# One semaphore for both producers of a scattered pair, and the other gathers held back behind the second expert's two tiles

## The chip, the cores and the metric

The kernel runs on one core of a Trainium2 chip. The metric is device time in microseconds for one execution; lower is better. Before the change, three runs took 111.3, 111.6 and 111.39 us, a median of 111.39.

## The reference, cut to what matters

Two layers, all in float32, with B = 4 sequences of S = 256 tokens and width H = 256.

```python
x = x + xattn(layernorm(x), ctx, Wq, bq, Wk, bk)    # attention among the 256 context rows mixes the columns of x
x = x + ffn(layernorm(x), gate_weight, wi, wo)

# ffn: T = 1024 tokens, E = 8 experts, capacity C = 160 rows for each
logits = tokens @ gate_weight.T
probs = softmax(logits)
mask = one_hot(argmax(logits), E)
ranks = cumsum(mask, axis=0) - 1                # place of a token in its expert's queue
mask = mask * (ranks < C)                       # tokens beyond the capacity are dropped
hmid = gelu(dispatch @ wi)                      # (8, 160, 256) x (8, 256, 1024)
eout = hmid @ wo                                # (8, 160, 1024) x (8, 1024, 256)
out = sum over experts of weight * eout         # each token gets its own row back
```

## The kernel before, in words

The program is written out by hand: each engine has its own list of instructions, and semaphores join them. Tokens are handled in 8 tiles of 128 rows, two tiles (a pair b, tiles 2b and 2b+1) for each sequence.

**Front part.** Attention and the first residual give `rows[:, n, 0:256]`, the new x of tile n. Beside it in `rows` stand four more columns: mean, reciprocal standard deviation, token index and softmax sum. For each pair VectorE ranks the tokens (`ranks`, `place`, L556 to L566) and writes `slot`, the place of each token's row in a table `slots_dram` in HBM of 8 x 160 rows of 1040 bytes. ScalarE's `expz(b)` (L394 to L399) writes the softmax sum. POOL makes the reciprocal standard deviation in `second_rstd(b)` (L300 to L304) and writes the rows of tile n to their slots with an indirect DMA, `scatter(n)` (L306 to L316). POOL's order is written out in L318 to L340: second_rstd(0), shifted_input(7), scatter(0), second_rstd(1), scatter(1), second_rstd(2), scatter(2), scatter(3), second_rstd(3), scatter(4) to scatter(7). The table is first filled with a constant row (L226, semaphore `filled`). Before the first scatter of a pair POOL waits for the slots (`slot_done`) and for the softmax sums (`zs_done`); scatter(0) waits for `filled` too. All eight scatters add to `scattered`.

**Expert 0** does not need the table: TensorE gathers its tokens by one-hot matrix products (`disp`), and the expert's first product starts from there.

**The other experts** read the table. SP waits for `scattered` (L232) and issues, one after the other and without a further wait: got_one (ranks 0 to 127 of expert 1, 130 KB), got_zero (expert 0, needed only for its output), got_main (experts 2 to 7, 780 KB in one DMA, 128 runs of 6240 bytes), rest_here[1] (ranks 128 to 159 of experts 4 to 7), the four stores of x to the output (`x1_out`), two more pieces of ranks 128 to 159 for the outputs (`last_slots`), and the weights of experts 3 to 7 (L233 to L242). ScalarE issues rest_here[0] (ranks 128 to 159 of experts 0 to 3) itself, in its own order: ahead of the third gelu of expert 0, so after the second (L443 to L449). The weights of experts 0 to 2 were loaded in the front part.

**Order on VectorE and TensorE.** `load_tile(i)` (L692 to L706) takes input tile i from the gathered rows and normalises it into `stok`; TensorE turns it with two transposes, `dT(i)` (L918 to L926, the matmuls of L778), and `load_tileT(i)` copies it to `dispT`. Input tile 0 is expert 1's (waits for got_one), tile 1 is rest_here[0]'s, tiles 2 and 3 are experts 2 and 3 (wait for got_main), tile 4 is rest_here[1]'s. `mm1(e)` is the first product of expert e: 16 block products, each of which the profile shows as two matmuls, in three groups of 12, 12 and 8 matmuls (L928 to L944). `mm2(e)` is the second product (L952 to L962). The transposes are placed inside: dT(0) and dT(1) ahead of the last quarter of mm2(0), dT(2) between the second and the third group of mm1(1), dT(3) ahead of mm1(2). The order is (L985 to L998):

```python
            mm1(0)
            mm2(0, next(outs), then=INS_AT[0])
            mm1(1, then=INS_AT[1])
            for s in range(2, E + 1):
                for i in INS_AT[s]:
                    dT(i)
                if s < E:
                    mm1(s)
                mm2(s - 1, next(outs))
```

`out_tile(n)` (L720 to L740) scales and adds the output of an expert's tile, and POOL scatters it to the output rows (L342 to L348); the first of these waits until all of `x1_out` has landed.

Of the kernel before, what the change touches and what calls it, by code (L numbers as in the profile page):

```python
# [5 lines left out]
ALU = mybir.AluOpType  # L6
ACT = mybir.ActivationFunctionType
AX = mybir.AxisListType
# [5 lines left out]
B = 4  # L14
# [15 lines left out]
MEAN, RSTD, INDEX, WEIGHT = H, H + 1, H + 2, H + 3  # L30
# [17 lines left out]
def xattn_moe(nc, x_in_v, xT_v, ctxT_v, small_v, wi_v, wo_v, out):  # L48
# [5 lines left out]
    with ExitStack() as stack:  # L54
        def sb(name, shape, dt=F32):
            return stack.enter_context(nc.sbuf_tensor(name, shape, dt))

        def sem(name):
            return stack.enter_context(nc.semaphore(name))
# [12 lines left out]
        def part(at, size, pattern, **sizes):  # L72
# [16 lines left out]
        rows = sb("rows", [P, NT, ROW])  # L89
# [30 lines left out]
        ranked = sb("ranked", [P, B, 2, E])  # L120
        slot = sb("slot", [P, NT], I32)
# [34 lines left out]
        fill_done, filled = sem("fill_done"), sem("filled")  # L156
# [8 lines left out]
        scaled_done, logits_done, lmax_done = sem("scaled_done"), sem("logits_done"), sem("lmax_done")  # L165
        below_done, val_done, vmax_done, mask_done = (sem("below_done"), sem("val_done"), sem("vmax_done"),
                                                      sem("mask_done"))
        rk_done, rank_read, slot_f_done, slot_done = (sem("rk_done"), sem("rank_read"), sem("slot_f_done"),
                                                      sem("slot_done"))
        bn2_done, st2_done, veps2_done = sem("bn2_done"), sem("st2_done"), sem("veps2_done")  # L170
        rstd2_done, zs_done, share_done = sem("rstd2_done"), sem("zs_done"), sem("share_done")
        warm_done = sem("warm_done")
        index_done, end_done = sem("index_done"), sem("end_done")
        tok_done, onehot_done = sem("tok_done"), sem("onehot_done")
# [2 lines left out]
        got_zero, got_one, got_main = sem("got_zero"), sem("got_one"), sem("got_main")  # L177
        got_rem = [sem(f"got_rem{r}") for r in range(STACKS)]
        rest_here = [sem(f"rest_here{r}") for r in range(STACKS)]
# [15 lines left out]
        @block.sync  # L195
        def _(sp):
            def context(i):
                a, z = CHUNKS[i]
                sp.dma_start(ctxT[:, a:z, :], ctxT_v[a:z].rearrange("b c s -> c b s")).then_inc(ctx_here[i], 16)  # L199

            def inputs(i):
                sp.dma_start(x_sb[:, 4 * i:4 * i + 4, :], x_in_v[i]).then_inc(x_here[i], 16)  # L202

            def turned_inputs(i):
                sp.dma_start(xT[:, 2 * i:2 * i + 2, :, :], xT_v[i]).then_inc(xT_here[i], 16)

            def weights(e):
                sp.dma_start(wi_sb[:, e, :, :], wi_v[e]).then_inc(wi_here[e], 16)
                sp.dma_start(wo_sb[:, e, :, :], wo_v[e]).then_inc(wo_here[e], 16)

            def last_slots(r):
                first = r * PER_STACK
                sp.dma_start(got[:, E + r, :],
                             by_rank[P:CAP, first:first + PER_STACK, :].rearrange("q j w -> j q w")
                             ).then_inc(got_rem[r], 16)

            context(0)
            context(1)
            inputs(0)
            context(2)  # L220
            turned_inputs(0)
            inputs(1)
            turned_inputs(1)

            sp.wait_ge(fill_done, 2)
            sp.dma_start(slots_dram.rearrange("(n p) r -> p n r", p=P),  # L226
                         fill[:, None, :].to_broadcast([P, E * CAP // P, ROW])).then_inc(filled, 16)
            weights(0)
            weights(1)
            weights(2)  # L230

            sp.wait_ge(scattered, 16 * NT)  # L232
            sp.dma_start(got[:, 1, :], by_rank[0:P, 1, :]).then_inc(got_one, 16)  # L233
            sp.dma_start(got[:, 0, :], by_rank[0:P, 0, :]).then_inc(got_zero, 16)
            sp.dma_start(got[:, 2:E, :], by_rank[0:P, 2:E, :]).then_inc(got_main, 16)
            sp.dma_start(rest[:, 1, :], by_rank[P:CAP, PER_STACK:E, :]).then_inc(rest_here[1], 16)
            for b in range(B):
                sp.dma_start(out_v[b], rows[:, 2 * b:2 * b + 2, 0:H]).then_inc(x1_out, 16)
            last_slots(0)
            last_slots(1)  # L240
            for e in range(3, E):
                weights(e)  # L242

        @block.gpsimd
        def _(pool):
# [53 lines left out]

            def second_rstd(b):  # L300
                pool.wait_ge(veps2_done, b + 1)
                pair = slice(2 * b, 2 * b + 2)
                nc.gpsimd.tensor_tensor(rows[:, pair, RSTD], rows[:, pair, RSTD], minus_half[:, 0:2],
                                        ALU.pow).then_inc(rstd2_done, 1)  # L304

            def scatter(n):  # L306
                if n == 0:
                    pool.wait_ge(slot_done, 1)
                    pool.wait_ge(zs_done, 2)
                    pool.wait_ge(filled, 16)  # L310
                elif n % 2 == 0:
                    pool.wait_ge(zs_done, n + 2)
                    pool.wait_ge(slot_done, n // 2 + 1)
                nc.gpsimd.indirect_dma_start(  # L314
                    slots_dram, bass.IndirectOffsetOnAxis(ap=slot[:, n:n + 1], axis=0), rows[:, n, :], None,
                    bounds_check=last_slot, oob_is_err=False).then_inc(scattered, 16)  # L316
# [9 lines left out]
            shifted_input(5)  # L326
            shifted_input(6)
            second_rstd(0)
            shifted_input(7)
            scatter(0)  # L330
            second_rstd(1)
            scatter(1)
            second_rstd(2)
            scatter(2)
            scatter(3)
            second_rstd(3)
# [23 lines left out]
        def _(act):  # L360
# [33 lines left out]
            def expz(b):  # L394
                act.wait_ge(below_done, b + 1)
                act.wait_ge(rstd2_done, b + 1)
                for n in range(2 * b, 2 * b + 2):
                    nc.scalar.activation(ez[:, n, :], below[:, b, n % 2, :], ACT.Exp, scale=rows[:, n, RSTD:RSTD + 1],  # L398
                                         accum_out=rows[:, n, WEIGHT:WEIGHT + 1]).then_inc(zs_done, 1)  # L399

            def token(n):

# [17 lines left out]
            exp(3)  # L420
            at(2)
            expz(0)
            token(0)
            at(3)
            expz(1)
            token(1)
            token(2)
            token(3)
            expz(2)
            token(4)  # L430
            token(5)
# [20 lines left out]
        def _(dve):  # L452
# [8 lines left out]
            def pair_of(b):  # L461
                return slice(2 * b, 2 * b + 2)
# [99 lines left out]
            def place(b):  # L562

                dve.wait_ge(rank_read, b + 1)
                nc.vector.tensor_reduce(slot_f[:, pair_of(b)], ranked[:, b, :, :], AX.X, ALU.max).then_inc(slot_f_done, 1)
                nc.vector.tensor_reduce(slot[:, pair_of(b)], ranked[:, b, :, :], AX.X, ALU.max).then_inc(slot_done, 1)  # L566

            def pick(n):

# [66 lines left out]
            ranks(0)  # L636
            summed(1)
            place(0)
            largest(1)
            x1(3)  # L640
# [18 lines left out]
            pick(0)  # L659
            pick(1)  # L660
            place(1)
            value(2)
            pick(2)
# [14 lines left out]
            ranks(2)  # L678
            first(3)
            place(2)  # L680
            chosen(3)
            pick(4)
# [347 lines left out]
```

## Time and profile before

| | |
|---|---|
| median of three runs | 111.39 us (111.3 to 111.6) |
| the profiled execution | 112.25 us |
| its span, first to last instruction | 110.5 us |
| TensorE matmuls busy | 102.0 us, 92% of the span |
| VectorE, ScalarE, POOL busy | 34.6, 31.5, 31.1 us |
| mean DMA rate over the span | 233 GB/s |

The profile shows one execution by the hardware profiler. PE is TensorE, PEld its weight loads, DVE VectorE, ACT ScalarE, POOL GpSimd, SP the engine that issues most DMAs. An engine name with q (SPq, ACTq, POOLq) is that engine's sequencer: the time of a DMA issue there is the issue alone, and not the transfer. L233 is line 233 of the kernel. Times are from the first instruction on.

### The profile page before, as it was taken

What the parts mean: (1) busy time and instruction counts of PE and PEld (TensorE: products, weight loads), DVE (VectorE), ACT (ScalarE), POOL (GpSimd) and SP (SyncE); (2) the same over time, 40 slices, a digit from 0 to 9 for tenths busy, and PEclk for the clock granted to TensorE, in tenths of its full rate; (3) what the DMA queues carried; (4) which work ended last, traced back from release to release, by engine and by line L of the source; (5) the groups of instructions that cost most, each with busy time, mean ns of one, the idle gap of its engine ahead of it and who ended that gap; (6) DMA issues with size and microseconds to landing.
All of it is one profiled execution on the core that took longest, in us unless ns stands there. A gap on an engine that the chain in (4) does not pass through costs nothing.

```text
span 110.5 us, 1990 instructions
## 1 busy us (share of the span) xinstructions
PE 102.0 (92%) x758; PEld 89.8 (81%) x758; DVE 34.6 (31%) x151; ACT 31.5 (29%) x81; POOL 31.1 (28%) x55
## 2 busy tenths in 40 slices
PE   5988999999799999999999999999999999999900
PEld 5565888678689989999999998669999999888800
DVE  0019899999930041800420400220020010012110
ACT  3247675367534302332031041002303204100000
POOL 5501388586775000030210210303002011031540
PEclk9999999999999999999999999999999999999995
DMA  2799999999973499999999999950001001001100
GB/s 76 225 336 371 352 296 421 427 415 414 423 278 120 122 279 371 304 309 411 428 424 415 427 421 424 427 190 16 0 0 41 6 0 47 0 0 46 56 3 3
DMA packets 7986, 25.77 MB, mean 233 GB/s; under 512 B 928, under 2 KB 4773, under 8 KB 5928
## 3 DMA queue, kind: packets, MB, share of 16 engines
q1 hardware_dynamic: 6664, 23.24, 56.3%
q0 software_dynamic: 880, 2.12, 5.2%
q10 hardware_dynamic: 432, 0.27, 0.9%
q8 instruction: 6, 0.10, 0.4%
q14 instruction: 4, 0.03, 0.1%
HBM read 21.14 MB, written 4.76 MB: 234 GB/s over the span
## 4 chain that ended last, share of the span: by engine, by line
PE 78%; DMA 6%; DVE 4%; ACT 4%; issue 3%; SPq 1%; POOL 1%; ACTq 0%; DVEq 0%
PE ps L781 71%; DMA shared<-in_ctxT 6%; PE ps L871 3%; ACT shared L406 2%; PE ps L778 2%; PE ps L824 1%; ACT ez L398 1%; DVE rows L516 1%; POOL out L353 1%; SPq L199 1%; DVE nmax L493 1%; ACT attended L366 0%; DVE stats L580 0%; SPq L202 0%; DVE y_end L757 0%
## 5 line engine op out<-in xcount | busy, mean ns | idle before, releaser
L781 PE MATMUL ps<-wo_sb,shared 128*32 128x128 f32 (+2 forms) x320 | 36.6, 337 | 0.0
L781 PE MATMUL ps<-shared,wi_sb 128*128 128x160 f32 x256 | 36.3, 299 | 0.3 <-issue 0.3
L781 PEld LDWEIGHTS ps<-shared,wi_sb 128*128 128x128 f32 x256 | 35.1, 190 | 0.6 <-issue 0.4
L781 PEld LDWEIGHTS ps<-wo_sb,shared 128*32 128x32 f32 (+1 forms) x320 | 29.4, 142 | 5.1 <-issue 1.0
L448 ACT ACTIVATE shared<-ps 128x480 f32<-128x480 f32 (+1 forms) x24 | 12.6, 526 | 48.2 <-PE ps L781 48.2
L346 POOL DMA_INDIRECT out<-y,got x9 | 8.7, 971 | 59.3 <-DVE y L739 44.1
L739 DVE SCALAR_TENSOR_TENSOR y<-ps,share,got 128x256 f32<-128x256 f32 x9 | 4.4, 484 | 48.1 <-PE ps L781 24.7
L314 POOL DMA_INDIRECT slots_dram<-rows,slot x8 | 8.2, 1028 | 4.0 <-issue 1.4
L781 PE MATMUL ps<-attended,shared 128*128 128x272 f32 x32 | 8.4, 402 | 0.2 <-ACT attended L366 0.2
L781 PEld LDWEIGHTS ps<-attended,shared 128*128 128x128 f32 x32 | 5.7, 189 | 1.4 <-ACT attended L366 0.3
L871 PE MATMUL ps<-shared 128*128 128x160 f32 x32 | 5.3, 309 | 0.6 <-ACT shared L406 0.6
L781 PE MATMUL ps<-shared,small 128*128 128x256 f32 (+1 forms) x12 | 5.1, 542 | 0.8 <-DMA shared<-in_ctxT 0.7
L705 DVE TENSOR_SCALAR stok<-got 128x256 f32<-128x256 f32 x7 | 2.7, 415 | 9.0 <-DMA got<-slots_dram 9.0
L871 PEld LDWEIGHTS ps<-shared 128*128 128x128 f32 x32 | 4.6, 190 | 1.0 <-ACT shared L406 0.8
L472 DVE BATCH_NORM_STATS2 stats<-shared 128x6 f32<-128x256 f32 x8 | 3.0, 414 | 6.9 <-DMA shared<-in_x 6.9
L781 PEld LDWEIGHTS ps<-shared,small 128*128 128x128 f32 x12 | 2.4, 230 | 2.8 <-DMA shared<-in_ctxT 1.4
L824 PEld LDWEIGHTS ps<-turner,shared 128*128 128x128 f32 x32 | 4.2, 190 | 0.3
L824 PE MATMUL ps<-turner,shared 128*128 128x136 f32 x32 | 4.4, 279 | 0.0
L384 ACT ACTIVATE shared<-ps,nmax 128x256 f32<-128x256 f32 x8 | 3.7, 469 | 2.0 <-DVE nmax L493 2.0
L297 POOL TENSOR_SCALAR shared<-shared,shift 128x256 f32<-128x256 f32 x8 | 4.0, 508 | 0.4 <-DVE shift L488 0.4
L781 PE MATMUL ps<-shared 128*128 128x256 f32 x16 | 4.0, 384 | 0.0
L366 ACT ACTIVATE attended<-ps 128x264 f32<-128x264 f32 x8 | 3.0, 390 | 3.6 <-PE ps L824 3.5
(82 smaller groups left out, 77.4 us busy)
## 6 DMA issues: line engine op xcount, KB each, us to landing
wi_sb<-in_wi SPq DMA_DIRECT2D x8, 1024.0 KB, 16.6
wo_sb<-in_wo SPq DMA_DIRECT2D x8, 1024.0 KB, 16.7
slots_dram<-fill SPq DMA_DIRECT2D x1, 1300.0 KB, 13.1
shared<-in_x SPq DMA_DIRECT2D x2, 512.0 KB, 7.4
shared<-in_xT SPq DMA_DIRECT2D x2, 512.0 KB, 8.2
out<-rows SPq DMA_DIRECT2D x4, 256.0 KB, 5.4
got<-slots_dram SPq DMA_DIRECT2D x1, 780.0 KB, 6.6
got<-slots_dram SPq DMA_DIRECT2D x4, 130.0 KB, 2.4
```

The costliest lines, as they stand in the source:

```text
L297: nc.gpsimd.tensor_scalar(x_sb[:, n, :], x_sb[:, n, :], 1.0, shift1[:, n:n + 1], ALU.mult, ALU.add).then_inc(xs_done, 1)
L314: nc.gpsimd.indirect_dma_start(slots_dram, bass.IndirectOffsetOnAxis(ap=slot[:, n:n + 1], axis=0), rows[:, n, :], None, bounds_check=last_ ...
L346: nc.gpsimd.indirect_dma_start(out_rows, bass.IndirectOffsetOnAxis(ap=got[:, t, INDEX:INDEX + 1].bitcast(I32), axis=0), y[:, n % 2, :], No ...
L366: return nc.scalar.activation(dst, src, ACT.Copy)
L384: nc.scalar.activation(att[:, b, m, :], p_en[b][:, m * S:(m + 1) * S], ACT.Exp, bias=nmax[:, n:n + 1], accum_out=esum[:, n:n + 1]).then_in ...
L448: nc.scalar.activation(gelu[:, e % RING, a:z, :], p_h[j][:, 0:(z - a) * CAP], ACT.Gelu).then_inc(gelu_done, 1)
L472: nc.vector.bn_stats(stats[:, 0, n, :], x_sb[:, n, :]).then_inc(bn1_done, 1)
L705: nc.vector.tensor_scalar(stok[:, i % 2, :], row[:, 0:H], row[:, MEAN:MEAN + 1], row[:, RSTD:RSTD + 1], ALU.subtract, ALU.mult).then_inc(s ...
L739: nc.vector.scalar_tensor_tensor(y[:, n % 2, :], p_o[n % 2][:, 0:H], share[:, t:t + 1], got[:, t, 0:H], ALU.mult, ALU.add).then_inc(y_done, 1)
L781: return nc.tensor.matmul(dst, lhsT, rhs, start=(k == 0), stop=last)
L824: last = nc.tensor.matmul(p_at[c][:, E + m * P:E + m * P + HALF], att[:, b, m, c * P:(c + 1) * P], turner[:, b % 2, m * HALF:(m + 1) * HAL ...
L871: last = nc.tensor.matmul(p_disp[c], tok[:, n, c * P:(c + 1) * P], onehot[:, n, :], start=(n == 0), stop=(n == NT - 1))
```

## The change

Three edits. The semaphores `zs_done` and `slot_done` are replaced by one for each pair, `row_ready[b]`, to which ScalarE adds twice and VectorE once, and the scatter of an even tile waits for 3 of it. The wait for `filled` moves from scatter(0) to second_rstd(0). On SP, two waits are put in behind the issue of got_one: one for got_one itself and one for rest_here[0]; got_zero, got_main and everything behind them are issued after that.

```diff
--- before.py
+++ after.py
@@ -165,10 +165,10 @@
         scaled_done, logits_done, lmax_done = sem("scaled_done"), sem("logits_done"), sem("lmax_done")
         below_done, val_done, vmax_done, mask_done = (sem("below_done"), sem("val_done"), sem("vmax_done"),
                                                       sem("mask_done"))
-        rk_done, rank_read, slot_f_done, slot_done = (sem("rk_done"), sem("rank_read"), sem("slot_f_done"),
-                                                      sem("slot_done"))
+        rk_done, rank_read, slot_f_done = sem("rk_done"), sem("rank_read"), sem("slot_f_done")
         bn2_done, st2_done, veps2_done = sem("bn2_done"), sem("st2_done"), sem("veps2_done")
-        rstd2_done, zs_done, share_done = sem("rstd2_done"), sem("zs_done"), sem("share_done")
+        rstd2_done, share_done = sem("rstd2_done"), sem("share_done")
+        row_ready = [sem(f"row_ready{b}") for b in range(B)]
         warm_done = sem("warm_done")
         index_done, end_done = sem("index_done"), sem("end_done")
         tok_done, onehot_done = sem("tok_done"), sem("onehot_done")
@@ -231,6 +231,9 @@
 
             sp.wait_ge(scattered, 16 * NT)
             sp.dma_start(got[:, 1, :], by_rank[0:P, 1, :]).then_inc(got_one, 16)
+
+            sp.wait_ge(got_one, 16)
+            sp.wait_ge(rest_here[0], 16)
             sp.dma_start(got[:, 0, :], by_rank[0:P, 0, :]).then_inc(got_zero, 16)
             sp.dma_start(got[:, 2:E, :], by_rank[0:P, 2:E, :]).then_inc(got_main, 16)
             sp.dma_start(rest[:, 1, :], by_rank[P:CAP, PER_STACK:E, :]).then_inc(rest_here[1], 16)
@@ -299,18 +302,16 @@
 
             def second_rstd(b):
                 pool.wait_ge(veps2_done, b + 1)
+                if b == 0:
+                    pool.wait_ge(filled, 16)
                 pair = slice(2 * b, 2 * b + 2)
                 nc.gpsimd.tensor_tensor(rows[:, pair, RSTD], rows[:, pair, RSTD], minus_half[:, 0:2],
                                         ALU.pow).then_inc(rstd2_done, 1)
 
             def scatter(n):
-                if n == 0:
-                    pool.wait_ge(slot_done, 1)
-                    pool.wait_ge(zs_done, 2)
-                    pool.wait_ge(filled, 16)
-                elif n % 2 == 0:
-                    pool.wait_ge(zs_done, n + 2)
-                    pool.wait_ge(slot_done, n // 2 + 1)
+
+                if n % 2 == 0:
+                    pool.wait_ge(row_ready[n // 2], 3)
                 nc.gpsimd.indirect_dma_start(
                     slots_dram, bass.IndirectOffsetOnAxis(ap=slot[:, n:n + 1], axis=0), rows[:, n, :], None,
                     bounds_check=last_slot, oob_is_err=False).then_inc(scattered, 16)
@@ -396,7 +397,7 @@
                 act.wait_ge(rstd2_done, b + 1)
                 for n in range(2 * b, 2 * b + 2):
                     nc.scalar.activation(ez[:, n, :], below[:, b, n % 2, :], ACT.Exp, scale=rows[:, n, RSTD:RSTD + 1],
-                                         accum_out=rows[:, n, WEIGHT:WEIGHT + 1]).then_inc(zs_done, 1)
+                                         accum_out=rows[:, n, WEIGHT:WEIGHT + 1]).then_inc(row_ready[b], 1)
 
             def token(n):
 
@@ -563,7 +564,7 @@
 
                 dve.wait_ge(rank_read, b + 1)
                 nc.vector.tensor_reduce(slot_f[:, pair_of(b)], ranked[:, b, :, :], AX.X, ALU.max).then_inc(slot_f_done, 1)
-                nc.vector.tensor_reduce(slot[:, pair_of(b)], ranked[:, b, :, :], AX.X, ALU.max).then_inc(slot_done, 1)
+                nc.vector.tensor_reduce(slot[:, pair_of(b)], ranked[:, b, :, :], AX.X, ALU.max).then_inc(row_ready[b], 1)
 
             def pick(n):
 
```

## Rows read from the trace of the kernel before

**Rows 1.** The page: busy time of the engines, and the DMA rate in 40 slices of the span

```profile
PE 102.0 (92%) x758; PEld 89.8 (81%) x758; DVE 34.6 (31%) x151; ACT 31.5 (29%) x81; POOL 31.1 (28%) x55
...
GB/s 76 225 336 371 352 296 421 427 415 414 423 278 120 122 279 371 304 309 411 428 424 415 427 421 424 427 190 16 0 0 41 6 0 47 0 0 46 56 3 3
```

**Rows 2.** Windows: stretch, us, busy PE, PEld, DVE, ACT, POOL, PEclk, DMA share, GB/s

```profile
32.70:105.70 73.00, 72.42 (x594) 66.15 (x594) 11.52 (x36) 13.80 (x25) 11.57 (x12) 1.00 0.54 202
```

**Rows 3.** Timeline of TensorE, 28 to 70 us: start, us, line, operation, count

```profile
41.04 3.42 PE L781 MATMUL ps<-shared,wi_sb 128*128 128x160 f32 x24
44.30 0.38 PE L778 MATMUL ps<-idg,stok 128*128 128x128 f32 x2
...
45.83 4.51 PE L781 MATMUL ps<-shared,wi_sb 128*128 128x160 f32 x32
...
54.07 4.51 PE L781 MATMUL ps<-shared,wi_sb 128*128 128x160 f32 x32
```

**Rows 4.** Timeline of VectorE, 30 to 70 us; in brackets the idle time before and its releaser

```profile
38.46 0.41 DVE L705 TENSOR_SCALAR stok<-got 128x256 f32<-128x256 f32 x1 [6.08 <-DMA got<-slots_dram]
39.22 0.41 DVE L705 TENSOR_SCALAR stok<-rest 128x256 f32<-128x256 f32 x1 [0.34 <-DMA rest<-slots_dram]
...
43.77 0.73 DVE L705 TENSOR_SCALAR stok<-got 128x256 f32<-128x256 f32 x2 [2.92 <-DMA got<-slots_dram]
```

**Rows 5.** Timelines of SP (fill, gathers, weights of expert 3) and of ScalarE

```profile
4.34 1.01 SPq L226 DMA_DIRECT2D slots_dram<-fill  x1
...
36.35 0.33 SPq L233 DMA_DIRECT2D got<-slots_dram  x1
36.72 0.43 SPq L234 DMA_DIRECT2D got<-slots_dram  x1
37.20 0.49 SPq L235 DMA_DIRECT2D got<-slots_dram  x1
...
43.28 0.50 SPq L208 DMA_DIRECT2D wi_sb<-in_wi  x1
...
36.26 0.57 ACT L448 ACTIVATE shared<-ps 128x480 f32<-128x480 f32 x1 [1.06 <-PE ps L781]
36.36 0.57 ACTq L446 DMA_DIRECT2D rest<-slots_dram  x1
```

**Rows 6.** DMA issues, us to landing: fill, got_main; issues at 36.35; at 36.72; at 43.28

```profile
slots_dram<-fill SPq DMA_DIRECT2D x1, 1300.0 KB, 13.1
...
got<-slots_dram SPq DMA_DIRECT2D x1, 780.0 KB, 6.6
...
got<-slots_dram SPq DMA_DIRECT2D x1, 130.0 KB, 2.1
rest<-slots_dram ACTq DMA_DIRECT2D x1, 130.0 KB, 2.8
...
got<-slots_dram SPq DMA_DIRECT2D x1, 130.0 KB, 2.8
...
wi_sb<-in_wi SPq DMA_DIRECT2D x1, 1024.0 KB, 8.5
```

**Rows 7.** DMA packets that started from 38.60 to 41.75 us, and from 41.75 to 43.70

```profile
DMA packets 300, 0.90 MB, mean 284 GB/s; under 512 B 34, under 2 KB 181, under 8 KB 300
...
DMA packets 706, 0.72 MB, mean 371 GB/s; under 512 B 47, under 2 KB 697, under 8 KB 706
```

**Rows 8.** Timelines of POOL (second_rstd(0), scatter(0), scatter(4)) and VectorE (slots of pairs 0, 2)

```profile
18.95 0.70 POOL L303 TENSOR_TENSOR rows<-rows,minus_half 128x2 f32<-128x2 f32 x1 [0.29 <-DVE rows L590]
...
21.29 1.22 POOL L314 DMA_INDIRECT slots_dram<-rows,slot  x1 [1.17 <-DVE slot L566]
...
29.99 1.04 POOL L314 DMA_INDIRECT slots_dram<-rows,slot  x1 [0.75 <-ACT ez L398]
...
20.82 0.16 DVE L566 TENSOR_REDUCE slot<-ranked 128x2 int32<-128x16 f32 x1
...
29.05 0.16 DVE L566 TENSOR_REDUCE slot<-ranked 128x2 int32<-128x16 f32 x1
```

## The prediction

> **What bounds the kernel now.** I read the busy shares first, then the chain of waits, then the windows. TensorE is busy for 92% of the span [rows 1], and the chain that ended last says the same of the path to the end: nearly all of it is matmuls. From 32.70 us, where the first expert starts, to the last matmul at 105.70, TensorE is busy for 72.42 us of 73.00 at a granted clock of 1.00 of full speed, its 2.4 GHz level [rows 2]. So in this stretch nothing that comes earlier can help unless TensorE waits for it, and anything that TensorE waits for moves the end by as much. The other half of the reading is therefore a search for the place where a later gather would be felt.
>
> That place is the second expert's first matrix product, mm1(1). After its 24th matmul TensorE turns tile 2, which is a part of the large gather got_main (L235). The two transposes start at 44.30 us [rows 3]. The 32 matmuls of expert 2 take 4.51 us, 0.141 each with the last one draining; 24 of them from 41.04 end at 44.4, and the transposes may begin while the last one drains: TensorE came there just on time, without having stood. VectorE had waited 2.92 us for got_main, began at 43.77 and made tile 2 in half of 0.73 to the first 0.41 us, that is by 44.18 [rows 4]. The margin is about 0.1 us. **got_main is already the gather that ends last, with hardly any slack.** The second expert's own two tiles are not: VectorE has made them by 38.87 and 39.63 [rows 4], and TensorE, busy all the time with mm1(0) and the first matmuls of mm2(0) [rows 2], takes them up when it comes to them; making them earlier gives nothing.
>
> **The change part by part.**
>
> *One semaphore for a pair.* In the kernel before, scatter(n) of an even n waits twice, and the first of two waits is an instruction of its own. Scatter(0), whose last wait hangs on the scatter itself, starts at 21.29, and its slot was written at 20.82 + 0.16 = 20.98: 0.31 us. Scatter(4) starts at 29.99 while its slot was written at 29.05 + 0.16 = 29.21: 0.78 us [rows 8]. With one wait I price scatter(2) and scatter(4) at 0.3 instead of 0.75, so 0.45 us earlier each. They don't add up, since each is bound by its own slot. Scatters 5 to 7 follow scatter(4) at POOL's own pace, and the last one's data land 0.45 earlier: `scattered` comes at 35.9 instead of 36.35 [rows 5, 8]. The bounds are 0 (the wait costs nothing) and 0.5. On the path to the end this is worth nothing by itself: what it releases are the gathers, which TensorE doesn't wait for up to this point.
>
> *The wait for the fill, moved ahead of second_rstd(0).* The fill is issued at 4.34 and takes 13.1 us [rows 5, 6], so it has landed by 17.5; second_rstd(0) starts at 18.95 [rows 8]. Cost 0, with 1.5 us of cover. Without that cover, what is queued behind it on POOL (shifted_input(7), all the scatters) and ScalarE's expz(0) would slip by whatever the fill is late. The extra wait instruction there is at most 0.1 us, and shifted_input(7), which nobody needs for some microseconds, takes it up.
>
> *The two waits on SP.* Ahead of got_zero, SP now waits for got_one and for rest_here[0]. The latter is issued by ScalarE, in order behind the second gelu of expert 0: that gelu starts at 36.26 and the issue is at 36.36 [rows 5]. It can't follow `scattered` to 35.9; I put it at 36.3. got_one took 2.1 us to land and rest 2.8, both issued in the same instant [rows 6]. Now rest stands half a microsecond behind got_one and has no got_zero beside it. Between 2.1 and 2.8 I take 2.4: landing at 38.7. SP then issues got_zero at 38.7 and got_main 0.48 later (37.20 less 36.72 [rows 5]) at 39.2, instead of 37.20. **got_main is issued 2.0 us later.** Bounds of its issue: 38.9 (2.1) and 39.6 (2.8).
>
> *How long got_main takes.* It took 6.6 us [rows 6]. The packet counts show why: of its 128 packets (those from 2 KB to 8 KB: 300 - 181 = 119, and 706 - 697 = 9) 119 had started by 41.75, and the last 9 took until 43.7 [rows 7]. Most of the DMA engines were through two microseconds before the last one or two. Lower bound for the changed kernel: 2.1 us of got_one, plus 0.67 MB more at the 424 GB/s or so that the page's DMA slices reach [rows 1], so 1.6 us: 3.7 us, if no engine lags. Upper bound: 6.6 again. What disappears is the queueing: got_zero took 2.8 where got_one took 2.1 [rows 6], 0.7 us for standing behind rest and got_one. The nearest row is got_main's own, so I take 6.6 - 0.7 = 5.9: landing at 45.1, against 43.75 before, 1.35 us later. Less the margin of 0.1: **TensorE stands 1.25 us in the middle of mm1(1).**
>
> The Trainium skill speaks against this term. Its page "DMA: Bandwidth & Descriptors", section "Anatomy of one DMA — SWDGE (gpsimd) path", fits a DMA as 2.0 us plus its bytes over 436 GB/s. By an estimate from that page a gather of 0.8 MB takes 3.8 us, lands at 43.0, and the stall would be nothing; the trace doesn't agree for the gather before (6.6 us), which has other transfers beside it and is issued from SP.
>
> *What else moves with SP.* rest_here[1], the four x1 stores, the two last_slots and ten weight transfers are all issued up to 2.0 us later. rest_here[1] follows got_main and is needed one step later. POOL's first output scatter waits for x1_out and would start up to 2 us later; VectorE needs its buffer back only for output tile 2, which follows mm2(2) and so mm1(3), at 54.07 [rows 3]. The weights of expert 3 are issued at 43.28 and take 8.5 us, so 51.8 [rows 5, 6]; TensorE wants them at 54.07 [rows 3]. Two microseconds later is 53.8, still in time, and TensorE itself is then 1.25 later. Later weights come at a steadier distance. Cost 0; if the cover were gone it would be a few tenths at 54 us.
>
> *Sum.* 0 + 0 + 1.25 + 0. The profiled execution took 112.25 us with a span of 110.5, and lies 0.86 above the median of 111.39 of the three runs shown; a stall of TensorE adds the same to each, so I add it to the median: 111.39 + 1.25 = **112.6 us**. Differences under 0.3% (0.33 us) can't be told from none here.
>
> **The rivals.**
>
> *got_main lands in time (no change, 111.4 us).* The lag of an engine or two is chance, or comes from the small gathers running beside it, and with SP's pause it goes: 39.2 + 3.7 to 4.6 lands between 42.9 and 43.8. For it: 119 of the packets would have fitted in that time, and got_one and got_zero show no such lag. Against it: it needs a gather two microseconds shorter than the one seen, from the removal of two pieces of 130 KB. This is also where the skill's fit would put it. 0.25.
>
> *Faster (111.0 us).* POOL's 0.45 us reaches the front part: second_rstd(3) and with it ScalarE's expz(3) and token(7) come earlier, the dispatch ends earlier and the first expert starts up to 0.4 sooner. The time is 111.39 - 0.4 = 111.0 if no gather is late too. It decides if the last dispatch matmuls wait for POOL's work. Against it: the picks of pair 3 need slot 3, which comes from VectorE and TensorE alone, and the scatters are not read before 36 us. 0.08.
>
> *The full shift (113.6 to 113.8 us).* rest takes 2.8 us again and got_main 6.6: issue at 39.6, landing 46.2, stall 2.35. It needs the queueing to be as before although two of the transfers are gone. 0.12, the upper end of the forecast's own mechanism.
>
> *The change does nothing:* impossible for the SP waits, since rest lands well after SP's next issue (39.2 against 36.72); possible for the semaphore, if the wait that disappears had no cost. That alters none of the times above.
>
> **How the numbers follow.** got_main late by more than can be measured: 0.55 around 112.6, and 0.12 for the full shift, together 0.67 slower. In time: 0.25, same. Faster: 0.08. The likeliest single case gives the time. The range reaches down to the case in time with a little of the front's gain, 111.2, and up to 113.6, and leaves out the worst of the full shift and most of the fast case.
>
> **What would show it.** In the timeline of SP, got_zero's issue at 38.4 to 39.2 and the weights of expert 3 near 45.3; in POOL's, scatter(4) near 29.5 and the three after it as much earlier; VectorE's wait for got before tile 2 some 1.3 us longer; in TensorE's waits a new row for the transposes L778 near 44.3, of 1.0 to 1.5 us; every later stage shifted by just that. I'm wrong if got_main lands by 43.8, if TensorE's new idle time stands elsewhere (at the weights of expert 3, at 54 us), or if the first expert no longer starts at 32.7.

## The result: slower by 1.1%, and the profile after

The kernel after takes 112.91 us (median of 6 runs, 112.42 to 113.62), the kernel before 111.61 (6 runs): a ratio of 1.0109 with a 95% interval of 1.0077 to 1.0142, which is 1.2 us (the two medians are 1.3 us apart). The profiled execution after took 112.42 us with a span of 110.7, the lowest of its six. Some executions of most kernels here, the one before too, are 1 to 6 us longer than the rest; the ratios leave them out, and where the profiled one was such an execution the text says so. Line numbers below are those of each kernel.

TensorE's waits after, whole kernel: who waited for what, us in total, times, longest. The last row is of the kernel before.

```profile
...
PE ps L782 <- DVE shared L691: 1.0, 1, 1.0
PE ps L872 <- issue: 0.4, 1, 0.4
PE ps L862 <- DVE mask L554: 0.2, 1, 0.2
PE ps L779 <- DVE stok L706: 0.2, 1, 0.2
...
PE ps L781 <- DMA shared<-in_ctxT: 0.7, 1, 0.7
```

Two of these were not there before: 1.02 us ahead of expert 0's first product (0.26 before), and a wait for tile 2. The profiled execution before stood 0.7 us for an input (ctxT) near its start, and the one after did not. So their spans, 110.5 and 110.7 us, lie closer together than the medians, and what follows counts from the start of expert 0 or from the last warm-up matmuls ahead of it. The timeline of TensorE has both:

```profile
31.10 0.38 PE L786 MATMUL ps<-warm_w 128*128 128x128 f32 x2
32.50 4.58 PE L782 MATMUL ps<-shared,wi_sb 128*128 128x160 f32 x32 [1.02 <-DVE shared L691]
...
40.81 3.42 PE L782 MATMUL ps<-shared,wi_sb 128*128 128x160 f32 x24
44.42 0.44 PE L779 MATMUL ps<-idg,stok 128*128 128x128 f32 x2 [0.18 <-DVE stok L706]
...
54.24 4.51 PE L782 MATMUL ps<-shared,wi_sb 128*128 128x160 f32 x32
```

From the start of expert 0 to the transposes of tile 2 it is 44.42 - 32.50 = 11.92 us. Before it was 11.57 (44.30 [rows 3] less the 32.73 at which expert 0 starts there). So TensorE lost 0.35 us to got_main, though the idle time is shown as 0.18 (the record of the matmuls before it, 40.81 + 3.42 = 44.23, runs past the moment at which the transposes could have begun, as it did before). From there to mm1(3) nothing is lost that was not lost before (9.82 us here, 9.77 in [rows 3]): the weights of expert 3 are in time.

SP and ScalarE, the counterpart of [rows 5], and how long the gathers took, that of [rows 6]:

```profile
34.95 0.33 SPq L233 DMA_DIRECT2D got<-slots_dram  x1
38.64 0.33 SPq L237 DMA_DIRECT2D got<-slots_dram  x1
39.01 0.43 SPq L238 DMA_DIRECT2D got<-slots_dram  x1
...
44.94 0.56 SPq L208 DMA_DIRECT2D wi_sb<-in_wi  x1
...
36.03 0.57 ACT L449 ACTIVATE shared<-ps 128x480 f32<-128x480 f32 x1 [1.06 <-PE ps L782]
36.04 0.57 ACTq L447 DMA_DIRECT2D rest<-slots_dram  x1
```

```profile
got<-slots_dram SPq DMA_DIRECT2D x1, 780.0 KB, 4.9
...
rest<-slots_dram ACTq DMA_DIRECT2D x1, 130.0 KB, 2.5
```

The small gather of ScalarE is issued right behind its second gelu and takes 2.5 us; SP goes on at 38.64. Counted from the start of expert 0, got_main is issued at 6.51 us instead of 4.47, 2.04 later, and takes 4.9 us instead of 6.6. VectorE begins tile 2 at 43.95:

```profile
31.34 0.32 DVE L691 TENSOR_SCALAR shared<-ps 128x160 f32<-128x160 f32 x1 [1.28 <-PE ps L872]
...
38.59 0.41 DVE L706 TENSOR_SCALAR stok<-rest 128x256 f32<-128x256 f32 x1 [1.13 <-DMA rest<-slots_dram]
...
43.95 0.74 DVE L706 TENSOR_SCALAR stok<-got 128x256 f32<-128x256 f32 x2 [3.33 <-DMA got<-slots_dram]
```

POOL and ScalarE after, the counterpart of [rows 8]: second_rstd(0), scatter(4), scatter(6), and ScalarE's copy of expert 0's tokens.

```profile
18.13 0.70 POOL L308 TENSOR_TENSOR rows<-rows,minus_half 128x2 f32<-128x2 f32 x1 [0.29 <-DVE rows L591]
...
28.52 1.04 POOL L315 DMA_INDIRECT slots_dram<-rows,slot  x1 [0.37 <-DVE slot L567]
...
31.20 0.97 POOL L315 DMA_INDIRECT slots_dram<-rows,slot  x1 [0.30 <-issue]
...
32.05 0.30 ACT L438 ACTIVATE shared<-ps 128x160 f32<-128x160 f32 x1 [2.63 <-PE ps L872]
```

From second_rstd(0) to scatter(4) it is 10.39 us, 11.04 before: 0.65 us gained, and the idle time ahead of scatter(4) fell from 0.75 to 0.37. Counted as the prediction counts, from the slot (written at 28.07 + 0.16 = 28.23) to the scatter, it is 0.29 instead of 0.78 us. second_rstd(0) waits no longer than before (0.29), so the fill costs nothing there. But scatter(6) now starts 0.1 us behind the start of the warm-up matmuls that follow the dispatch (31.10; it was 0.53 us before), and the two copies of the dispatch's result, which had followed it at once before, come late: ScalarE's starts 0.95 us after that row's 31.10 (0.20 before), VectorE's 0.24 us after it. ScalarE's late copy, which ends at 32.35, is what TensorE stands for in the 1.02 us; the row names VectorE's, but that had ended at 31.66. It had no place in the prediction.

The merge also brought a gain on TensorE's path. Tile 3 of the dispatch, the 4 matmuls ahead of which TensorE waits, and VectorE's one-hot rows for it (`pick(3)`), each before and after:

```profile
28.71 0.78 PE L871 MATMUL ps<-shared 128*128 128x160 f32 x4 [0.61 <-ACT shared L406]
...
27.72 0.78 PE L872 MATMUL ps<-shared 128*128 128x160 f32 x4 [0.43 <-issue]
...
28.02 0.54 DVE L575 TENSOR_SCALAR shared<-first_slots,slot_f,rows 128x160 f32<-128x160 f32 x1
...
27.21 0.36 DVE L576 TENSOR_SCALAR shared<-first_slots,slot_f,rows 128x160 f32<-128x160 f32 x1
```

pick(3) took 0.54 us and TensorE waited 0.61 us in all three traces with two semaphores for a pair (before, e1, e3 below); it is 0.36 and 0.43 us in all eleven with one. So the front part is about 0.2 us shorter with the merge. Before, pick(3) ran beside POOL's scatter(3), which is now all but over when it starts (26.28 + 0.97 = 27.25); that this makes it faster is not shown.

### The profile page after: what moved, and what is told of

Read it like the earlier page. It is cut to its first block, busy times and chain, and to the rows that moved or that the text cites. A ratio compares the mean times of both kernels' runs of the same rounds, so it can differ in the third digit from the quotient of the medians.

```text
span 110.7 us, 1988 instructions
## 1 busy us (share of the span) xinstructions
PE 102.1 (92%) x758; PEld 89.9 (81%) x758; DVE 34.5 (31%) x151; ACT 31.4 (28%) x81; POOL 31.2 (28%) x55
## 4 chain that ended last, share of the span: by engine, by line
PE 80%; DMA 7%; DVE 5%; issue 3%; POOL 1%; ACT 1%; SPq 0%; DVEq 0%; ACTq 0%
PE ps L782 69%; PE ps L872 4%; DMA got<-slots_dram 4%; DMA rest<-slots_dram 2%; PE ps L786 2%; PE ps L779 2%; PE ps L825 1%; DVE rows L517 1%; POOL out L354 1%; ACT attended L367 1%; DVE nmax L494 1%; DVE stats L581 0%; PE ps L856 0%; DVE stok L706 0%; DVE y_end L758 0%
## 6 DMA issues: line engine op xcount, KB each, us to landing
slots_dram<-fill SPq DMA_DIRECT2D x1, 1300.0 KB, 12.7
```

## The experiments

Twelve runs were made on three chips, four on each; the first pair (before and after, above) is called chip 1 (it may be one of the others), and the runs e1 to e4 are chip 2, e5 to e8 chip 3, e9 to e12 chip 4. Each ratio is against the kernel before on the same chip. The last three columns are from each trace: TensorE's idle time ahead of expert 0; the time from the start of expert 0 to the transposes of tile 2, less 11.57; and got_main from issue to landing.

| run | what | ratio, 95% interval | gap, us | lost to gathers, us | got_main, us |
|---|---|---|---|---|---|
| (chip 1) | before, after | 1.0109 (1.0077 to 1.0142) | 0.26, 1.02 | 0, 0.35 | 6.6, 4.9 |
| e1 | before | 1.0011 (0.9992 to 1.003) | 0.27 | 0 | 5.4 |
| e2 | semaphore only | 0.9999 (0.9973 to 1.0025) | 0.26 | 0 | 6.4 |
| e3 | SP waits only | 1.0065 (1.0042 to 1.0088) | 0.26 | 0.37 | 4.7 |
| e4 | after, got_main ahead of the waits | 1.0124 (1.0093 to 1.0155) | 0.26 | 1.99 | 4.8 |
| e5 | after | 1.0106 (1.006 to 1.0152) | 1.13 | 0.52 | 5.1 |
| e6 | after, got_main ahead of got_zero | 1.0048 (1.0019 to 1.0076) | 1.12 | 0 | 4.2 |
| e7 | after, expert 2's rows ahead of the waits | 1.0081 (1.0049 to 1.0113) | 1.11 | 0 | 4.3 (650 KB) |
| e8 | after, wait for got_one only | 1.0082 (1.0053 to 1.0111) | 1.12 | 0 | 5.2 |
| e9 | semaphore only | 0.998 (0.9947 to 1.0013) | 0.26 | 5.08, see below | 6.3 |
| e10 | after, scatter(6) held | 1.0076 (1.0047 to 1.0106) | 0.26 | 1.12 | 4.6 |
| e11 | after | 1.0045 (1.0018 to 1.0071) | 0.26 | 0.74 | 5.1 |
| e12 | after, scatter(6) held | 1.0123 (1.0077 to 1.0168) | 0.26 | 1.15 | 4.6 |

### e1 to e3: the two halves of the change apart

e1 is the kernel before, unchanged.

> The kernel before, unchanged, for a second trace. The first trace of it (112.25 us) was 0.64 above its median; I expect about 111.5 us (ratio 1.000 within 0.3%), with the front part 0.5 to 0.9 us shorter than in the first trace because ctxT lands at 7.8 us instead of 8.6, as it does in the trace after the change. Theory A (got_main is late) expects no idle time of TensorE ahead of the transposes at 44 us and got_main landing within 6 to 7 us of its issue. Theory B (something at the start of expert 0 is late) expects TensorE to go from the dispatch to expert 0 within 0.5 us, where the trace after the change shows 1.02 us.

Measured 110.77 us against 110.88. The trace has the gap of 0.27 us and no wait for a gather; got_main took 5.4 us here, less than I expected, so the 6.6 us of the first trace was at the long end. With it VectorE could begin tile 2 at 41.54 and TensorE came to it at 43.19: the margin, 0.1 us in the first trace, was 43.19 - (41.54 + 0.41) = 1.2 us here.

e2 takes the change without the two waits on SP.

```diff
-            sp.wait_ge(got_one, 16)
-            sp.wait_ge(rest_here[0], 16)
```

> The merged semaphore and the moved wait for the fill, with SP as before (no waits). Theory A, that the whole loss is got_main issued about 2 us later: as before, 111.4 to 111.8 us. Theory B, that the scatters moved earlier collide with the end of the dispatch and delay the start of expert 0 by 0.7 us, the gathers costing only the rest: 112.2 to 112.4 us.

Measured 1.000. On this chip the merged semaphore costs nothing, and the 0.2 us of the front part are within the interval. One of the twelve executions left out took 115.67 us; e9 comes back to that.

e3 is the kernel before with these two lines added.

> The two waits on SP alone, with both semaphores of the pair as before. Theory A: as slow as the whole change or slower, 112.8 to 113.2 us, because got_one starts about 0.9 us later while the small gather of ScalarE starts at the same time and has got_one beside it again. Theory B: 112.0 to 112.2 us.

Measured 1.0065, 0.7 us: between the two theories. The waits on SP alone cost this, and the trace has the cost in one place, the transposes of tile 2:

```profile
31.55 4.58 PE L784 MATMUL ps<-shared,wi_sb 128*128 128x160 f32 x32 [0.26 <-ACT shared L440]
...
43.49 0.44 PE L781 MATMUL ps<-idg,stok 128*128 128x128 f32 x2 [0.20 <-DVE stok L708]
```

11.94 us from one to the other, 0.37 more than before. That trace is of the fastest of its runs (110.59 us, against a median of 111.35), so the usual loss is probably larger.

### e4: got_main in front, and a wait that takes the place of the other

```diff
             sp.dma_start(got[:, 1, :], by_rank[0:P, 1, :]).then_inc(got_one, 16)
+            sp.dma_start(got[:, 2:E, :], by_rank[0:P, 2:E, :]).then_inc(got_main, 16)
             sp.wait_ge(got_one, 16)
             sp.wait_ge(rest_here[0], 16)
             sp.dma_start(got[:, 0, :], by_rank[0:P, 0, :]).then_inc(got_zero, 16)
-            sp.dma_start(got[:, 2:E, :], by_rank[0:P, 2:E, :]).then_inc(got_main, 16)
```

> The whole change, but got_main is issued right behind got_one and ahead of the two waits; only got_zero and what follows it are held back. Theory A: all of the loss goes, 111.4 to 111.7 us. Theory B: 112.2 to 112.4 us. Theory C, that the loss is in what is held back later (x1 stores, weights of expert 3 at 54 us): 112.6 to 113.0 us, with idle time of TensorE at 54 us.

All three theories missed it by place if not by size: 1.0124. TensorE no longer waits for tile 2 but for tile 1, ScalarE's small gather. Timeline of TensorE, then the issues at 35.35 us with their time to landing:

```profile
38.82 0.38 PE L779 MATMUL ps<-idg,stok 128*128 128x128 f32 x2
40.97 0.44 PE L779 MATMUL ps<-idg,stok 128*128 128x128 f32 x2 [1.77 <-DVE stok L706]
```

```profile
got<-slots_dram SPq DMA_DIRECT2D x1, 780.0 KB, 4.8
rest<-slots_dram ACTq DMA_DIRECT2D x1, 130.0 KB, 5.1
```

The same 130 KB that took 2.5 us behind the waits took 5.1 us beside got_main. The two were issued within 0.01 us, on two queues. The Trainium skill says why this can be ("DMA: Bandwidth & Descriptors", "Issuing engines are not separate DMA queues"): DMAs of SP and of ScalarE run on the same 16 DMA engines and interleave. This trace agrees: the small one landed last, 0.3 us after the large. So another queue gave the small gather no precedence over the large one.

### e5 to e8: where got_main has to be

e5 is the kernel after once more.

> The kernel after, unchanged, for a second trace. Theory A (the loss is the wait of TensorE for got_main): ratio to the kernel before 1.006 to 1.012, a gap of 0.26 us between the dispatch and expert 0, as in all other traces but the first one after the change (1.02 us), and idle time ahead of the transposes of tile 2. Theory B (the merged semaphore and the SP waits together delay the start of expert 0): the gap of about 1.0 us is there again.

1.0106, as in the first comparison, and both losses are in the trace: theories A and B each had half of it. Timeline of all engines at the start of expert 0:

```profile
31.66 0.38 PE L786 MATMUL ps<-warm_w 128*128 128x128 f32 x2
31.77 0.97 POOL L315 DMA_INDIRECT slots_dram<-rows,slot  x1 [0.30 <-issue]
32.68 0.32 DVE L691 TENSOR_SCALAR shared<-ps 128x160 f32<-128x160 f32 x1 [2.06 <-PE ps L872]
32.73 0.30 ACT L438 ACTIVATE shared<-ps 128x160 f32<-128x160 f32 x1 [2.74 <-PE ps L872]
...
33.17 0.37 PE L782 MATMUL ps<-shared,wi_sb 128*128 128x160 f32 x1 [1.13 <-issue]
```

VectorE and ScalarE start their copies 1.0 and 1.1 us behind the start of the warm-up matmuls, about when scatter(6) ends (32.74). In e1, without the gap, they do so 0.1 us ahead and 0.2 us behind.

e6 exchanges two lines behind the waits, so that got_main is issued at once and got_zero behind it.

> The kernel after with got_main issued ahead of got_zero behind the two waits, so 0.37 to 0.45 us earlier. Theory A: 0.3 to 0.5 us faster than the kernel after. Theory C (what counts is what stands further back, the x1 stores or the weights): as the kernel after, within 0.1%.

e7 gives expert 2's rows a semaphore of their own.

```diff
+            sp.dma_start(got[:, 2, :], by_rank[0:P, 2, :]).then_inc(got_two, 16)
             sp.wait_ge(got_one, 16)
             sp.wait_ge(rest_here[0], 16)
...
-            sp.dma_start(got[:, 2:E, :], by_rank[0:P, 2:E, :]).then_inc(got_main, 16)
+            sp.dma_start(got[:, 3:E, :], by_rank[0:P, 3:E, :]).then_inc(got_main, 16)
```

> The kernel after, but the rows of expert 2 (130 KB) are taken out of got_main and issued behind got_one, ahead of the two waits; all else is held back as in the kernel after. Theory A: the loss goes, ratio to the kernel before 0.998 to 1.003, no idle time of TensorE at the transposes. Theory C: the whole loss stays, 1.006 to 1.012. A small gather in front of ScalarE's does not delay it as the large one did (5.1 us to landing): I expect 2.8 to 3.2 us.

e8 leaves out `sp.wait_ge(rest_here[0], 16)`.

> The kernel after without the wait for rest_here[0]; SP waits for got_one alone. got_main is then issued about 1.1 us earlier than in the kernel after. With the 4.7 to 4.9 us that it took behind the waits, theory A expects it some 0.7 us ahead of need: ratio to the kernel before 0.998 to 1.003. But if ScalarE's small gather, still under way then, is slowed by it as it was by the large gather issued at the same time, TensorE waits for tile 1 at 38.8 us instead, and the ratio is 1.003 to 1.010.

In all three the wait for tile 2 is gone: transposes 11.57 us behind the start of expert 0, as before. For e8:

```profile
32.36 4.58 PE L781 MATMUL ps<-shared,wi_sb 128*128 128x160 f32 x32 [1.12 <-issue]
...
43.93 0.38 PE L778 MATMUL ps<-idg,stok 128*128 128x128 f32 x2
```

That settles theory A's part: the wait is for the rows of expert 2 and nothing else, and everything further back (got_zero, the stores of x, the weights) may stay held back as it is. The ratios, 1.0048 to 1.0082, didn't fall to 1.000, which theory A expected for e7 and e8. The gap ahead of expert 0 stood in all of them: 1.12 - 0.26 = 0.86 us, or 0.7 us less the gain of the front part, 0.6% of 111.8. That lies in the intervals of all three. No trace of the kernel before was taken on this chip; that it has no such gap here is inferred from these ratios. e6 is the lowest, 0.54 us, and 0.57 below e5's median. e8's ratio falls into the range of its second case, but not by that mechanism: the small gather took 2.5 us and TensorE did not wait for tile 1. In e7 it took 2.7 us with two gathers of 130 KB issued ahead of it, so small gathers in front did not hold it up.

### e9 to e12: the gap, and the dose

e9 is e2 again, to see whether the semaphore alone makes the gap on a chip that shows it.

> The merged semaphore and the moved wait for the fill alone, once more, because the gap of 1.1 us between the dispatch and expert 0 stood in all traces of kernels with POOL's earlier scatters on one chip and in none on another. Theory D (the earlier scatter(6), which now starts 0.1 us after TensorE's last dispatch matmul, delays what DVE and ScalarE hear of that matmul, on such chips): here, without any wait on SP, the gap is 1.1 us again, 0.85 more than before, and the ratio 1.006 to 1.008. Theory A (only got_main matters): gap 0.26 us, ratio 1.000. On a chip that does not show the gap, both expect 1.000.

The chip did not show it: gap 0.26 us, ratio 0.998. So this question stays open. But 7 of its 13 runs took 111.64 to 116.14 us, against 2 of 19 above 111.3 for the kernel before; the ratio leaves these out, and the median of all 13, 111.64, is 0.87 us above that of the kernel before. The profiled execution (115.5 us) was one of the seven. It shows the collision of e4 again, without any move of got_main in the program. The issues of SP and ScalarE, the small gather's time to landing, then TensorE:

```profile
35.08 0.33 SPq L233 DMA_DIRECT2D got<-slots_dram  x1
35.45 0.43 SPq L234 DMA_DIRECT2D got<-slots_dram  x1
35.92 0.43 SPq L235 DMA_DIRECT2D got<-slots_dram  x1
...
35.36 0.57 ACTq L444 DMA_DIRECT2D rest<-slots_dram  x1
```

```profile
rest<-slots_dram ACTq DMA_DIRECT2D x1, 130.0 KB, 6.5
```

```profile
42.40 0.44 PE L776 MATMUL ps<-idg,stok 128*128 128x128 f32 x2 [3.19 <-DVE stok L703]
...
43.54 5.10 PE L779 MATMUL ps<-shared,wi_sb 128*128 128x160 f32 x24
```

With the table complete earlier, SP issues its gathers earlier, while ScalarE's own still stands behind the second gelu. got_main is issued 0.56 us behind rest here; rest then took 6.5 us and TensorE waited 3.19. In the first trace and in e1, where got_main was 0.84 us behind it, rest took 2.8 us, and in e2, at 0.83 us, 3.0. So to be issued first was not enough at 0.56 us. These are single traces, and e9 and e2 are the same kernel. That the other six long executions have this cause is not shown. The next 24 matmuls took 5.10 us instead of 3.42: the windows (columns as in [rows 2]) show a mean granted clock of 0.66 over these 5 us (a mix of the 2.4 and the 1.2 GHz level), where it had been 1.00 before and during the idle time.

```profile
39.20:42.40 3.20, 0.01 (x2) 0.00 (x1) 0.47 (x2) 0.00 (x0) 0.00 (x0) 1.00 0.95 325
...
43.50:48.50 5.00, 5.00 (x26) 4.97 (x26) 0.93 (x4) 0.57 (x1) 0.97 (x1) 0.66 1.05 336
```

e10 and e12 are the kernel after with one more wait on POOL.

```diff
                 if n % 2 == 0:
                     pool.wait_ge(row_ready[n // 2], 3)
+                if n == 6:
+                    pool.wait_ge(disp_sb, 2)
```

> The kernel after, but POOL waits ahead of scatter(6) until expert 0's tokens are copied (disp_sb at 2), so that this scatter starts behind the end of the dispatch as in the kernel before. Theory D: the gap goes back to 0.26 us; what is left is TensorE's wait for got_main, 0.2 to 0.5 us, ratio 1.002 to 1.006. If the gap has another cause (the place of the instructions in memory, the number of semaphores): gap 1.1 us still, ratio 1.009 to 1.012.

> The kernel after with scatter(6) held until expert 0's tokens are copied, once more. On a chip with the gap, theory D (the start of scatter(6) right behind TensorE's last dispatch matmul is what delays the next engines): gap 0.26 us, and 0.4 to 0.8 us faster than the kernel after. If the gap has another cause: 1.1 us again and no faster than the kernel after. On a chip without the gap: no faster than the kernel after, rather 0.1 to 0.3 us slower, since the table is complete 0.5 us later.

Chip 4 has no gap to take away, so neither run tests theory D; nor does e11 show one, with scatter(6) in the same place as in e5. Its timeline, to be read beside e5's:

> The kernel after once more, beside the next one. If this chip is of the kind that shows the gap of 1.1 us ahead of expert 0: ratio 1.009 to 1.012. If it is of the other kind (gap 0.26 us in every trace so far): the wait for got_main alone, ratio 1.005 to 1.008, as the SP waits alone gave there (1.0065).

```profile
31.36 0.32 DVE L691 TENSOR_SCALAR shared<-ps 128x160 f32<-128x160 f32 x1 [0.96 <-PE ps L872]
31.43 0.38 PE L786 MATMUL ps<-warm_w 128*128 128x128 f32 x2
31.54 0.97 POOL L315 DMA_INDIRECT slots_dram<-rows,slot  x1 [0.30 <-issue]
31.63 0.30 ACT L438 ACTIVATE shared<-ps 128x160 f32<-128x160 f32 x1 [1.87 <-PE ps L872]
```

As in e5 the scatter starts 0.11 us behind the warm-up matmuls, but both copies start at once. Without the gap the whole change costs 1.0045 here, 0.5 us, and TensorE's loss of 0.74 us in the trace (an execution 0.3 above its median) carries it all.

What e10 and e12 do give is a dose. Holding scatter(6) moved the table and both first gathers back by more than the 0.5 us I had reckoned with (rest is issued 4.5 us behind the start of expert 0 instead of 3.5), and with them got_main; e12 is 0.96 us slower than e11, not 0.1 to 0.3. Time of its issue behind the start of expert 0, and the loss: 4.5 us (e1), 0; 5.5 (e8), 0; 6.1 (e6), 0; 6.5 to 6.7 (the kernel after three times, e3), 0.35 to 0.74; 7.6 (e10, e12), 1.12 and 1.15, of which 0.5 is at tiles 0 and 1. Up to 6.1 us a later issue was free, with got_main taking 5.2 us in e8 and 4.2 us in e6, where got_zero stood behind it instead of ahead; beyond that it was paid.

## Why the prediction was right, and where it was not

The time, the range and the side were right: 112.6 us forecast from a median of 111.39, 1.25 us slower, and 1.2 us measured. The reason given was only half of it.

**The wait itself** is where I put it: TensorE stands at the transposes of tile 2, waiting for got_main, and nowhere behind. But it is the smaller part of the new idle time. By the prediction's own signs of being wrong (new idle time elsewhere, VectorE's wait 1.3 us longer) the forecast fails in part: more than half of it stands ahead of expert 0, and VectorE's wait grew from 2.92 to 3.33 us. e7 shows that it is these rows alone. SP's pause was right too: I had ScalarE's gather issued as soon as its gelu allows, landing after 2.4 us (2.5 measured), and got_main 2.0 us later (2.04).

**The term that was mis-sized** is how long got_main takes: "so I take 6.6 - 0.7 = 5.9". Behind the waits it took 4.9, 5.1 and 5.1 us in the three traces of the kernel after, so the stall was 0.35, 0.52 and 0.74 us instead of 1.25. Packet counts after, 40.00 to 43.10 us and 43.10 to 44.00:

```profile
DMA packets 278, 0.92 MB, mean 296 GB/s; under 512 B 31, under 2 KB 151, under 8 KB 278
...
DMA packets 328, 0.32 MB, mean 357 GB/s; under 512 B 21, under 2 KB 327, under 8 KB 328
```

127 of the 128 large packets had started by 43.10, and one came later, where before nine were left over for two microseconds [rows 7]. So the lag of single engines, on which the forecast leaned, was mostly gone; e1 and e2, without waits, had 5.4 and 6.4 us, so part of the 6.6 was chance, and with it the margin of 0.1 us (1.2 in e1). The rival in which it lands in time named this and went too far: 4.6 us would have been early enough, and it took longer in all three traces. The 3.8 us that the prediction works out from the Trainium skill ("DMA: Bandwidth & Descriptors", "Anatomy of one DMA — SWDGE (gpsimd) path") was reached by no run; the least is 4.2 (e6).

**The step that failed** is in the part on the semaphore: "On the path to the end this is worth nothing by itself". On chips 1 and 3 the kernels with the merged semaphore start expert 0 0.75 to 0.87 us late, in five traces of five, and the only trace of the kernel before on such a chip (the first one) does not; on chips 2 and 4 nothing of it is seen. The SP waits are reached more than 2 us later, so what they make SP do can't be the cause; the merge and the moved wait for the fill were never run apart, nor either of them without the SP waits on such a chip. The merge also gained: about 0.2 us on TensorE's path, in every trace that has it. I had a gain there as the rival *Faster*, by way of second_rstd(3); it came by VectorE's pick(3) and was half the size. So in the traces of chip 1 the terms are 0.76 us of the gap and 0.35 of got_main, less 0.2, where my sum has 0 and 1.25. They make 0.9 us, in the fastest of the six executions; the rest up to 1.2 is probably a longer wait for got_main in the others. **That the total agrees is mostly luck.** That the delay comes from scatter(6) standing right behind the dispatch is argued from the order of the rows only; the run that would show it, e10 or e12 on a chip with the gap, fell on one without.

**The small parts** held. Scatter(4) gained 0.49 us against its slot (forecast 0.45), the fill had landed (4.32 + 12.7 = 17.0, second_rstd(0) at 18.13), the weights of expert 3 were in time. The merge seems to have a second price that I did not name: it brings got_main closer behind ScalarE's gather (0.56 us in e9, 0.84 before). With the two waits on SP got_main comes later; rest took 2.5 to 2.7 us in every such trace but e4's, and on e9's chip 1 of 12 executions of the kernel after (e11) was long, against 7 of 13. No version run here beats the kernel before by more than the interval.

## What to carry to other kernels

When a transfer is held back for the good of others, look for its own first reader, count its margin there, and hold back only what has one: here all of the queue could wait except one expert's rows, or all of it by a microsecond but not by two. A DMA that is urgent should be issued well ahead of a large one, or alone: to be small and on another queue did not help it beside a large one, and neither did 0.56 us of lead in the one trace that had it; 0.83 us did. And a total that comes out as forecast doesn't show that its terms did: the trace has to be asked for each.

## What the runs showed that I had not expected

- 130 KB in runs of 1040 bytes took 2.5 us to land behind the waits and 5.1 us (e4) and 6.5 us (e9) with got_main issued at the same time and 0.56 us behind it on the other queue. With 0.83 to 0.84 us between them it took 2.8 to 3.0 us.
- With scatter(6) 0.10 to 0.12 us behind the start of the last warm-up matmuls, VectorE's and ScalarE's next steps came late on chips 1 and 3, which may be one and the same (ScalarE's by 0.75 to 0.87 us), and at once on chips 2 and 4. In all five late traces ScalarE's copy starts 0.01 to 0.12 us ahead of the end of that scatter; VectorE's does so in three, and in two (the first one and e7) it is only 0.3 to 0.4 us late. In e1, without any delay, ScalarE's copy starts as near to the end of scatter(5), so the coincidence alone proves nothing. The cause is open.
- VectorE's pick(3) took 0.54 us with two semaphores for a pair and 0.36 us with one, and TensorE's wait for that tile 0.61 and 0.43 us, in all fourteen traces.
- An idle time of TensorE of 3.19 us was followed by 5 us at a mean granted clock of 0.66 and cost another 1.7 us (e9); one of 1.77 us (e4) was not followed by any fall:

```profile
40.97:46.00 5.03, 5.03 (x35) 4.93 (x36) 2.14 (x7) 1.00 (x2) 0.00 (x0) 1.00 0.78 251
```
